# One more fixed slot in each scan step for a shared-out feed-forward stage (two-layer Mamba, MoE and attention kernel)

## The reference, cut to what matters

```
x = x + L0_attn(layernorm(x))   # in_proj, conv, silu, dt = softplus(...), selective scan, * silu(z), out_proj
x = x + L0_ffn(layernorm(x))    # shared MLP 128->512->128 plus 8 experts of the same size, two of them gated per token
x = x + L1_attn(layernorm(x))   # 16 heads, 2048 x 2048 scores
x = x + L1_ffn(layernorm(x))    # 8 experts, two per token
# the scan: 256 channels x 16 states, over time, in chunks of 32:
states = cum_dA * (h + cumsum(dBu / cum_dA));  y = (states * C).sum(over states)
```

## Time and profile before

| | |
|---|---|
| three runs | 1556.09, 1556.45, 1558.36 us; median 1556.45 |
| profiled execution | 1558.36 us, of which the span from first to last instruction is 1556.6 us |
| busy over the span | PE 84%, DVE 80%, ACT 67%, POOL 42% |
| mean granted TensorE clock | 0.917 |
| scan steps | 51 us (step 0) to 592 us (step 63) |
| from about 830 us | attention, with DVE and PE at 90% or more |

### The profile page before, as it was taken

The page is one execution under the profiler, slowest core; times in us unless marked ns, Lnnn a source line. Parts: engine busy times, 40 slices in busy tenths (PEclk is TensorE's granted clock), DMA queues, the critical chain, the costliest instruction groups (busy, mean ns, idle before and its releaser), DMA issues.

```text
span 1556.6 us, 22553 instructions
## 1 busy us (share of the span) xinstructions
PE 1307.7 (84%) x8408; PEld 506.7 (33%) x8408; DVE 1243.2 (80%) x1491; ACT 1039.3 (67%) x1821; POOL 661.3 (42%) x609
## 2 busy tenths in 40 slices
PE   4365659976985897888569999999999999999998
PEld 1111224433433343333212222222222222235963
DVE  0889988999899786456679999999999999943522
ACT  3542357755853663445239998999899988997653
POOL 0678867986787684744503112111111113111430
PEclk9666789997996998999759999999999999999999
DMA  7122213322321221223212011100010000000210
GB/s 219 66 65 81 68 49 96 88 69 75 81 75 54 81 75 31 55 68 50 33 54 50 29 29 48 22 2 2 2 23 2 2 2 19 6 26 13 75 31 27
DMA packets 63696, 75.71 MB, mean 49 GB/s; under 512 B 8633, under 2 KB 39226, under 8 KB 63458
## 3 DMA queue, kind: packets, MB, share of 16 engines
q1 hardware_dynamic: 62818, 72.70, 17.2%
q0 software_dynamic: 768, 1.57, 0.3%
HBM read 66.04 MB, written 8.21 MB: 48 GB/s over the span
## 4 chain that ended last, share of the span: by engine, by line
PE 44%; DVE 28%; issue 12%; POOL 11%; ACT 4%; DMA 1%; SPq 1%; DVEq 0%; POOLq 0%; ACTq 0%
DVE mx L1641 16%; PE PS L952 11%; PE PS L940 6%; PE PS L909 4%; DVE D L1430 3%; POOL D L1881 3%; PE PS L732 3%; PE PS L723 3%; PE PS L1024 2%; PE PS L1039 2%; DVE PS L1416 2%; POOL D L1897 2%; PE PS L1060 2%; PE PS L1048 2%; DVE PS L1422 2%
## 5 line engine op out<-in xcount | busy, mean ns | idle before, releaser
L1304 ACT ACTIVATE aa<-PS 128x512 f32<-128x512 f32 x1024 | 551.6, 598 | 57.6 <-PE PS L940 46.7
L1641 DVE TENSOR_REDUCE mx<-PS 128x2 f32<-128x1024 f32 x480 | 552.5, 1218 | 7.9 <-PE PS L909 5.1
L952 PE MATMUL PS<-aa,D 128*32 128x256 f32 x4096 | 321.6, 391 | 1.6 <-ACT aa L1304 0.6
L940 PE MATMUL PS<-D 54*128 54x512 bf16 x1024 | 212.0, 390 | 9.5 <-ACT aa L1304 8.9
L909 PE MATMUL PS<-D 51*128 51x512 bf16 x960 | 190.0, 385 | 17.5 <-DVE mx L1641 16.9
L1995 POOL CAST n<-nm 4x512 bf16<-4x512 f32 x15 | 9.0, 602 | 446.2 <-ACT nm L1286 446.2
L1416 DVE TENSOR_TENSOR_SCAN PS<-PS,D 128x512 f32<-128x512 f32 x128 | 157.5, 1230 | 10.3 <-POOL D L1897 3.5
L1194 ACT ACTIVATE HB<-PS 128x512 f32<-128x512 f32 x144 | 84.6, 596 | 114.9 <-PE PS L732 114.0
L732 PE MATMUL PS<-xnT,f_w 128*128 128x512 f32 x288 | 157.8, 641 | 2.4 <-ACT HB L1194 1.8
L1167 ACT ACTIVATE D<-D,Am 128x512 f32<-128x512 f32 x128 | 85.1, 713 | 97.8 <-DVE D L1430 95.9
L952 PEld LDWEIGHTS PS<-aa,D 128*32 128x32 f32 x4096 | 84.2, 108 | 191.9 <-issue 152.9
(11 more groups left out here) (326 smaller groups left out, 1771.2 us busy)
## 6 DMA issues: line engine op xcount, KB each, us to landing
D<-bc SPq DMA_DIRECT2D x128, 256.0 KB, 3.6
GB<-gd SPq DMA_DIRECT2D x32, 256.0 KB, 4.6
D<-sc SPq DMA_DIRECT2D x72, 64.0 KB
aa<-in_L_ffn_W SPq DMA_DIRECT2D x9, 256.0 KB, 3.4
D<-in_L_ffn_W SPq DMA_DIRECT2D x9, 256.0 KB, 3.5
f_w<-in_L_ffn_experts_w SPq DMA_DIRECT2D x1, 2048.0 KB, 9.3
f_w<-in_L_ffn_experts_w SPq DMA_DIRECT2D x8, 256.0 KB, 6.0
aa<-gh SPq DMA_DIRECT2D x1, 2048.0 KB, 9.3
```

Source lines behind the costliest of these rows:

```text
L940: e.matmul(take_exp(s + hh), KS[64 * hh:64 * hh + 54, p, 128 * kb:128 * kb + 128], QP[64 * hh:64 * hh + 54, qc % 2, p, :], start=True, sto ...
L952: t = e.matmul(PS[32 * j:32 * j + 32, 7, cs], va[:, kb, 9 * h:9 * h + 32], Pt[K % 3][:, 512 * j + 256 * n:512 * j + 256 * n + 256], start= ...
L1304: e.activation(Pt[K % 3][:, c:c + 512], bank((s + hh) % 3), ACT.Exp).then_inc(S("e_free"), 1)
L1641: e.tensor_reduce(mx4[:, G % 2, b, 2 * pair:2 * pair + 2, c:c + 1], max_banks(m), AX.X, ALU.max).then_inc(freed(m)[0], 1)
```

## The change

The condition of the third pull is taken away, so `sgen` is pulled four times in every step:

```
--- before.py
+++ after.py
@@ -107,8 +107,7 @@
         pull(sgen)
         if inside:
             p["mulW"](k, 1)
-        if k % 2 == 0 or k % 16 < 6:
-            pull(sgen)
+        pull(sgen)
         if inside:
             p["scanX"](k, 1)
             p["mulC"](k)
```

## The result

The changed kernel takes 1582.35 us in the median (1579.28 to 1585.06, four runs) against 1557.4 us before (1556.09 to 1558.58): ratio 1.016, 95% interval 1.0138 to 1.0182, some 25 us slower. Slower was forecast, by 14.6 us; the time lies above the range.

The account below looks back on a forecast made before the run. No engine bounds the whole span; TensorE bounds four-pull steps, VectorE by a little three-pull ones. Terms 5.9 + 5.9 + 0 + 2.8 = 14.6 us, on a median of 1556.45, gave 1571.0 us, range 1560 to 1578.

Parts of the forecast that it names:

- Its order in steps 30 to 32: First section: `gate_expert(7)` in step 30 ahead of `mulW(30, 1)`; `gate_expert(8)` in step 31 waits 1.3 us; `x_ffn` follows there.
- the length of step 32: Step 32, without `gate_expert(8)`, `x_ffn` and the 0.93 us wait, was to take 8.2 us instead of 10.1.
- the 0 of the third: Third section: steps 62 and 63 later, but the late chain behind step 63 gone; 0, bounds -2 and +2 us.
- the prediction's 589.6: Third section: the time in us at which step 63 was forecast to start; it was to end at 598.6.
- TensorE runs gaplessly, so its work isn't slowed: Steps 25 to 31: TensorE has no gap; only the scan step VectorE has reached when the ffn is done changes.
- item 1: First section: TensorE starts n = 33 at 304.7 instead of 306.12, one 1.72 us `sums` pair less, 0.3 added for ScalarE.
- 5.9: Loss in us forecast for each of sections one and two; in the first, step 33 starts at 326.7 against 320.84.
- ScalarE chokes in the full steps: Rival: silus queued behind exponentials give TensorE gaps, 2.5 us more in each of three sections, 1578.5 us; chance 0.10.
- full steps of 8.6 us: Steps with k % 16 = 8 to 14: four pulls and `sums` fill TensorE for 8.6 us each.
- The clock's 2.8 us: Convolution in step 33 starts at the slow clock, as in step 17; +2.8 us once, bounds 0 and 2.8.
- The tie of VectorE to TensorE: At `gate_expert`, VectorE waits for down matmuls (30.4 us before) and can't run ahead by more than one pull.
- a cover of 2.5 steps: Gate rows and exponentials of step k + 2 have over 20 us of cover, so their cost was set at nothing.

Follow-up runs that it names:

- the longer run with extra matmuls: The changed kernel with seven extra matmuls behind the sums of step 31 and one more between step 33's transposes and its convolution; ratio 1.0141.
- the shorter one: The changed kernel with six extra TensorE matmuls behind the sums of step 31; 1580.42 us, ratio 1.0152.
- the repeat: The changed kernel run once more with no edit; 1580.37 us, ratio 1.0148 against the kernel before.

## Why the prediction was wrong

- **Direction and most of the mechanism held.** In four-pull steps TensorE's list and not VectorE's work sets the length, VectorE idles (12.5 us in steps 25 to 31), and once the sub-steps are done VectorE has one step more to go. Its order in steps 30 to 32, the length of step 32 (8.20 against 8.2), the independence of the sections and the 0 of the third (+0.5) came out. In the third, step 63 starts 8.4 us later against step 56, where the prediction's 589.6 is 7.0 later.
- **The step that failed** is "TensorE runs gaplessly, so its work isn't slowed", and with it the term of item 1, 0.3 us a section for ScalarE. The rows behind it were of alternating steps, in which a three-pull step lets ScalarE catch up. In full steps the silus' turn behind two table loads and two exponentials makes TensorE wait 0.36 us in each plain step and more where the preparation shares ScalarE. TensorE's start of n = 33 came 2.9 us later than item 1 has it, and the sections measured 8.9 and 10.0 us instead of 5.9. With the table loads gone the two kernels differ by 5.4 and 5.8, and n = 33 stands where item 1 puts it. So the term set at 0.3 us was too small by 3 and 4 us; this is 7 of the 10 us by which the sum fell short of 25. The rival "ScalarE chokes in the full steps" named it, priced it at 2.5 us a section and was given 0.10. It had the loss in the third section too, where the end of the scan gives it back. The row of step 26, full and gapless, was taken for all full steps. The prediction isn't at one with itself here: it lists full steps of 8.6 us, while its items have 53.9 us (255.5 to 309.4) for steps 25 to 30, 9.0 each; they took 55.9.
- **The clock's 2.8 us** measured 2.6 (steps 33 to 36, 1.0 + 1.6), but as two things; that they add up to nearly the forecast is luck. The slow start came, with a first group of 5.23 us and a wait of 2.19 in step 36 where 6.4 and 3 were forecast. 1.9 us belong to the slow clock, shown by the longer run with extra matmuls (step 36 at 10.5 against 8.57; before it was 8.95, so against before 1.6 are left). By the Trainium skill's rule on the clock (TensorE: Matmul & The Clock Gate, "What's actually happening") activity releases it. The longer run agrees, with 1.00 over the first group; the shorter one, with 0.67, shows that activity some time before is not enough. The other 1.0 us, in step 33, is not the clock (last section).
- **The tie of VectorE to TensorE** at `gate_expert` is real (the kernel without it is 16 us nearer to before), but not the only one; the prediction set the exponentials at nothing with a cover of 2.5 steps. For the sum this changed nothing, since the first tie is the tighter.
- **Scope.** The stretches add up to 22.0 us (21.6 in the repeat, against 23.2 by the runs); the 1 to 3 us left lie behind the scan and are not explained.

## What to carry to other kernels

When side work is dealt out over the steps of a loop, the step's length is that of the longest engine in that step, or of a round trip between two, so in this kernel an even deal beats an early one, and two late extra pulls cost less (2.7 us) than two early ones (8.5). Before calling an engine gapless in a denser step, follow its buffers' round trip through the other engine in that step's own order: here 3.9 us of table loads and exponentials between two silus were hidden only as long as lighter steps lay between. A loss of a whole chain at the end can be free where another engine's queue was already the last one.

## What the runs showed of the hardware

A tiny VectorE operation can cost a microsecond beside GpSimd. The norm's shift (128x4) in step 33, in the kernel after, with GpSimd's `mulC` from 330.11 to 332.45:

```profile
331.28 1.20 DVE L1367 SCALAR_TENSOR_TENSOR shift<-mv,rstd 128x4 f32<-128x4 f32 x1
```

In the kernel before it took 0.15 us, and stood beside GpSimd's `clamp`, since `x_ffn` held VectorE back in step 32. Step 33 grew by this 1.0 us (7.80 to 8.79), and the convolution came 1.05 us later in it. The product without a PSUM operand shows the same (2.47 against 0.69). The Trainium skill (SBUF — State Buffer, "SBUF: two separate sides") says that a VectorE instruction with two SBUF inputs and a GpSimd instruction that reads SBUF exclude each other for the whole instruction. The ends agree: 331.28 + 1.20 = 332.48. No run here tests it by moving this instruction alone. Moving work can thus change the length of an instruction that isn't moved.

The clock can be back at 0.50 just behind dense work: with six extra matmuls TensorE worked from 326.06 to 332.4 and from 333.48 on, with 1.08 and 0.69 us of idle time between, and the next eight instructions still took 5.40 us. The granted clock was 1.00 from 328.2 to 334.9 and 0.50 from 335.0 to 338.3.

One kernel's attention stage differs from run to run more than its scan: 954.4 and 966.1 us behind `sums(63)` for the same program. In 400 us of it VectorE was busy 392.07 in one and 381.05 in the other; TensorE's granted clock was 1.00 in the one and 0.98 in the other. The two rows, of the repeat and of the first profile:

```profile
1000.00:1400.00 400.00, 384.85 (x4065) 106.15 (x4063) 392.07 (x406) 365.04 (x682) 61.21 (x72) 1.00 0.04 8
```

```profile
1013.50:1413.50 400.00, 380.84 (x3949) 103.46 (x3945) 381.05 (x395) 355.17 (x663) 61.16 (x72) 0.98 0.04 8
```

What starts the lower clock there is not settled.
